# Gathers of 127 and 125 rows, and PSUM operands for VectorE, in a two-layer graph kernel

## The reference

```
# layer 0
m     = relu(x[src] + edge_attr)                       # 400000 x 32
neigh = segment_sum(m, dst, num_segments=12500)
x     = layernorm(x + (1 + eps) * x + neigh)
# layer 1
x_s   = x * rsqrt(clip(out_degree, 1))[:, None]
agg   = segment_sum(x_s[src], dst, num_segments=12500)
x     = layernorm(x + agg * rsqrt(clip(in_degree, 1))[:, None])
```

## Time and profile before

| | |
|---|---|
| time, median of 2 runs | 6580.52 us (6580.47 to 6580.58) |
| the profiled execution | 6585.29 us, span 6583.5 us |
| first layer, to the end of its sums | 0 to 4763 us |
| norm between the layers | 4763 to 4820 us |
| second layer's sums | 4820 to 6540 us |
| final norm and output | 6540 to 6584 us |
| GpSimd (POOL) busy | 5088.2 us, 77% |
| VectorE (DVE) busy | 2819.4 us, 43% |
| TensorE (PE) busy | 2745.2 us, 42% |
| ScalarE (ACT) busy | 1588.2 us, 24% |
| mean granted TensorE clock | 0.684 |

### The profile page before, as it was taken

One profiled execution on the slowest core, in us unless ns is written; L12 is line 12 of the kernel. 1 busy time (PEld: TensorE's weight loads), 2 busy tenths in 40 slices (PEclk: granted clock), 3 DMA queues, 4 the chain that ended last, 5 costly groups with the idle time before them and its releaser, 6 DMA issues. The chain is left out here.

```text
span 6583.5 us, 68332 instructions
## 1 busy us (share of the span) xinstructions
PE 2745.2 (42%) x22843; PEld 2292.8 (35%) x22843; DVE 2819.4 (43%) x4668; ACT 1588.2 (24%) x2158; POOL 5088.2 (77%) x4335
## 2 busy tenths in 40 slices
PE   2222222222222222222222222222358888888887
PEld 2222222222222222222222222222347676666665
DVE  5233232232232232332232332332367777777776
ACT  0000000000000000000000000000068888888885
POOL 7787787787787787787787787787767777777773
PEclk7555555555555555655555655655679999999998
DMA  2111111111111111111111111111111111111111
GB/s 45 24 21 22 24 21 21 24 21 21 24 21 22 24 21 22 24 21 22 24 21 22 24 21 22 24 21 22 18 38 19 19 19 18 19 18 19 18 19 28
DMA packets 246365, 147.86 MB, mean 22 GB/s; under 512 B 159963, under 2 KB 229164, under 8 KB 245804
## 3 DMA queue, kind: packets, MB, share of 16 engines
q0 software_dynamic: 138400, 80.97, 9.0%
q1 hardware_dynamic: 107940, 66.58, 4.1%
HBM read 141.61 MB, written 5.61 MB: 22 GB/s over the span
## 5 line engine op out<-in xcount | busy, mean ns | idle before, releaser
L133 POOL DMA_INDIRECT rows<-in_x,src_t x3125 | 3796.8, 1215 | 957.6 <-issue 952.0
L380 PE MATMUL agg<-dst_hot,msg 128*33 128x128 f32 x6250 | 943.4, 326 | 2487.5 <-ACT msg L364 2487.5
L380 PEld LDWEIGHTS agg<-dst_hot,msg 128*33 128x33 f32 x6250 | 831.2, 136 | 2593.4 <-ACT msg L364 2514.5
L133 POOL DMA_INDIRECT rows<-table,src x1200 | 1279.1, 1066 | 387.2 <-issue 377.5
L578 ACT ACTIVATE counts<-built 128x686 bf16<-128x686 f32 x1925 | 1452.8, 984 | 261.8 <-PE built L603 252.0
L364 ACT ACTIVATE msg<-edge_t 128x800 f32<-128x800 f32 (+1 forms) x126 | 108.9, 864 | 4602.8 <-DVE edge_t L297 4602.8
L297 DVE TENSOR_TENSOR edge_t<-edge_t,rows 128x800 f32<-128x800 f32 (+1 forms) x126 | 125.5, 996 | 2109.0 <-DMA rows<-in_x,src_t 2109.0
L603 PE MATMUL built<-key_hot,hi_hot 128*128 128x343 bf16 x3850 | 930.5, 325 | 103.5 <-ACT counts L578 56.7
L622 PE MATMUL applied<-counts,x_parts 128*96 128x175 bf16 x7546 | 913.7, 246 | 0.9 <-ACT prod L583 0.9
L622 PEld LDWEIGHTS applied<-counts,x_parts 128*96 128x96 bf16 x7546 | 786.3, 128 | 152.9 <-ACT counts L578 1.0
L376 PE MATMUL hist<-lo_hot,hi_hot 128*128 128x98 bf16 x3125 | 277.8, 283 | 1003.5 <-DVE lo_hot L288 1003.5
(11 more groups left out here) (109 smaller groups left out, 702.6 us busy)
## 6 DMA issues: line engine op xcount, KB each, us to landing
edge_t<-in_edge_attr SPq DMA_DIRECT2D x125, 400.0 KB
rows<-in_x,src_t POOLq DMA_INDIRECT x3125, 2.4
rows<-table,src POOLq DMA_INDIRECT x1200
src_t<-in_src SPq DMA_DIRECT2D x125, 12.5 KB
dst_t<-in_dst SPq DMA_DIRECT2D x125, 12.5 KB
base_t<-in_dst SPq DMA_DIRECT2D x125, 0.5 KB
x<-x SPq DMA_DIRECT2D x1, 1568.0 KB
x<-in_x SPq DMA_DIRECT2D x1, 1372.0 KB
```

The costliest lines, as they stand in the source:

```text
L133: gp.indirect_dma_start(rows_d[:, j, :], None, nodes, bass.IndirectOffsetOnAxis(ap=src_d[:, j:j + 1].bitcast(U32), axis=0),).then_inc(s, 16)
L380: last = te.matmul(agg[:, :], msg[:, j, :], dst_hot[:, j, :], start=(j == 0), stop=(j == J - 1))
```

## The change

**First layer.** Groups 0 to 124 take M0 = 127 partitions (3175 edges), one last group, the 126th, takes M1 = 125 (3125 edges); every gather, comparison, addition and product of a group is on that many partitions. VectorE's comparisons read their integer row from PSUM (`iota_ps`, a copy made once) and not from SBUF. A ScalarE copy puts the group's edge rows into PSUM (`edge_ps`, signalled by `s_edge`), and the edge addition reads them there; it still writes into `edge_t`. The edge rows are loaded by two DMAs (partitions 0 to 111 and the rest), so `s_in` counts to 80 a group.

**Second layer.** NG = 80 groups of 16 gathers of 125 rows (160000 edges), and NC = 75 counted groups (240000 edges). `LAST` becomes 80. Since gathers now outlast the counted groups, waits for `l_moved` go by the helper `moves`. The comparisons there keep both operands in SBUF.

```diff
-    NG = 3 * J
-    NC = G - NG * JG // J
-    CE0 = NG * JG * P
+    M0, M1 = P - 1, P - 3
+    G0 = E // (M0 * J)
+    GE0, LAST0 = M0 * J, E - G0 * M0 * J
+    NG = 80
+    CE0 = NG * JG * M1
+    NC = (E - CE0) // GE
...
-            sp.dma_start(edge_d.rearrange("p j d -> p (j d)"),
-                         edge[bass.ds(e0, GE), :].rearrange("(p j) d -> p (j d)", p=P)).then_inc(s, 16)
+            for p0, p1 in bands:
+                sp.dma_start(edge_d[p0:p1, :, :].rearrange("p j d -> p (j d)"),
+                             edge[bass.ds(e0 + p0 * J, (p1 - p0) * J), :].rearrange("(p j) d -> p (j d)", p=p1 - p0)).then_inc(s, 16)
...
                 gp.indirect_dma_start(
-                    rows_d[:, j, :], None, nodes,
-                    bass.IndirectOffsetOnAxis(ap=src_d[:, j:j + 1].bitcast(U32), axis=0),
+                    rows_d[0:m, j, :], None, nodes,
+                    bass.IndirectOffsetOnAxis(ap=src_d[0:m, j:j + 1].bitcast(U32), axis=0),
...
+                iota_ps = pb("iota_ps")[:, 0:P]
+                edge_ps = own.enter_context(nc.psum_tensor("edge_ps", [P, 1024], F32))[:, 0:J * D].rearrange("p (j d) -> p j d", d=D)
+                s_edge = sem("s_edge")
...
+                    V(ve.tensor_copy(iota_ps, iota[:, :]))
...
+                            row = iota_ps[0:m, :].unsqueeze(1).to_broadcast([m, J, P])
...
-                            ve.tensor_tensor(hi_hot[:, :, :], tiles_of(iota[:, :], J), last_dim(s_hi[:, :], P), ALU.is_equal).then_inc(s_v, 1)
+                            ve.tensor_tensor(hi_hot[0:m, :, :], row, last_dim(s_hi[0:m, :], P), ALU.is_equal).then_inc(s_v, 1)
...
-                            ve.tensor_tensor(lo_hot[:, :, :], tiles_of(iota[:, :], J)[:, :, 0:C], last_dim(s_lo[:, :], C), ALU.is_equal).then_inc(s_v, 1)
-                            ve.tensor_tensor(dst_hot[:, :, :], tiles_of(iota[:, :], J), last_dim(rel[:, :], W), ALU.is_equal).then_inc(s_v, 1)
+                            ve.tensor_tensor(lo_hot[0:m, :, :], row[:, :, 0:C], last_dim(s_lo[0:m, :], C), ALU.is_equal).then_inc(s_v, 1)
+                            ve.tensor_tensor(dst_hot[0:m, :, :], row, last_dim(rel[0:m, :], W), ALU.is_equal).then_inc(s_v, 1)
...
+                                    ve.wait_ge(s_edge, g + 1)
...
-                                piece = edge_t[:, slot, j0:j1, :]
-                                ve.tensor_tensor(piece, piece, rows[:, slot, j0:j1, :], ALU.add).then_inc(s_v, 1)
+                                ve.tensor_tensor(edge_t[0:m, slot, j0:j1, :], edge_ps[0:m, j0:j1, :], rows[0:m, slot, j0:j1, :], ALU.add).then_inc(s_v, 1)
...
+                            sc.wait_ge(s_in[slot], (i + 1) * 80)
+                            sc.activation(edge_ps[0:m, :, :], edge_t[0:m, slot, :, :], ACT.Copy).then_inc(s_edge, 1)
...
-                            gathers(gp, 0, JG, table[:, :], rows[:, slot, :, :], src_t[:, slot, :], l_rows[slot])
+                            gathers(gp, M1, 0, JG, table[:, :], rows[:, slot, :, :], src_t[:, slot, :], l_rows[slot])
...
+            def moves(k):
+
+                return min(k - 1, NC + 1) if isinstance(k, int) else k - 1
```

More of the change, by code:

```diff
@@ L38, in build @@
     HS = [n * SPAN for n in HT]
-    assert G * GE == E and G % 2 == 1 and NC <= P and C % 2 == 0 and CE0 + NC * GE == E and CE0 % GE == 0
+    assert LAST0 == M1 * J and G0 % 2 == 1 and NC <= P and C % 2 == 0 and CE0 + NC * GE == E and CE0 % GE == 0
     assert 0 < TAIL <= C and HK <= 512 and max(HS) <= P and J % CH == 0 and J - 1 <= C and KEYS <= J * NC
@@ L180, in both @@
                     for slot in range(2):
-                        step(i, slot, i * 2 + slot)
-                step(turns, 0, G - 1)
+                        step(i, slot, i * 2 + slot, M0)
+                step(turns, 0, G0 - 1, M0)
+                step(turns, 1, G0, M1)
             with ExitStack() as own:
@@ L343, in _, with step @@
                             gp.iota(pick_i[:, h, :], [[1, max(HT)], [0, SPAN]], base=h * HT[0], channel_multiplier=0).then_inc(s_const, 1)
-                        def step(i, slot, g):
-                            gp.wait_ge(s_in[slot], (i + 1) * 64)
+                        def step(i, slot, g, m):
+                            gp.wait_ge(s_in[slot], (i + 1) * 80)
                             gp.sem_inc(s_mark, 1)
-                            n = PIECES[0][1] if isinstance(g, int) else J
-                            gathers(gp, 0, n, x[:, :], rows[:, slot, :, :], src_t[:, slot, :], s_rows[slot])
+                            n = PIECES[0][1] if m == M1 else J
+                            gathers(gp, m, 0, n, x[:, :], rows[:, slot, :, :], src_t[:, slot, :], s_rows[slot])
                             if n < J:
-                                gathers(gp, n, J, x[:, :], rows[:, slot, :, :], src_t[:, slot, :], s_late)
+                                gathers(gp, m, n, J, x[:, :], rows[:, slot, :, :], src_t[:, slot, :], s_late)
                         both(gp, step)
@@ L371, in _, with step @@
                         prepare_pe(te)
-                        def step(i, slot, g):
+                        def step(i, slot, g, m):
                             te.wait_ge(s_v, g * VG + (v0 + 6))
                             for j in range(J):
-                                te.matmul(hist[:, :], hi_hot[:, j, :], lo_hot[:, j, :], start=False, stop=False)
-                            for n, (j0, j1) in enumerate(PIECES if isinstance(g, int) else [(0, J)]):
+                                te.matmul(hist[:, :], hi_hot[0:m, j, :], lo_hot[0:m, j, :], start=False, stop=False)
+                            for n, (j0, j1) in enumerate(PIECES if m == M1 else [(0, J)]):
                                 te.wait_ge(s_a, g + (len(ROUNDS) + 1 + n))
                                 for j in range(j0, j1):
-                                    last = te.matmul(agg[:, :], msg[:, j, :], dst_hot[:, j, :], start=(j == 0), stop=(j == J - 1))
+                                    last = te.matmul(agg[:, :], msg[0:m, j, :], dst_hot[0:m, j, :], start=(j == 0), stop=(j == J - 1))
                             last.then_inc(s_agg, 1)
@@ L477, in step @@
                                 sp.wait_ge(l_hot, g - 1)
[L478 removed]
+                            load_indices(sp, g * (JG * M1), M1, JG, src_t[:, slot, :], dst_t[:, slot, :], base_t[:, slot, :], l_in[slot])
                         each(sp, step, NG - 1)
@@ L503, in dst_hots @@
                             def dst_hots(j0, j1):
-                                return ve.tensor_tensor(dst_hot[:, j0:j1, :], tiles_of(iota_b[:, :], j1 - j0),
-                                                        last_dim(rel[:, j0:j1], W), ALU.is_equal)
+                                return ve.tensor_tensor(dst_hot[0:M1, j0:j1, :], tiles_of(iota_b[:, :], j1 - j0)[0:M1, :, :],
+                                                        last_dim(rel[0:M1, j0:j1], W), ALU.is_equal)
                             def chunk(q):
@@ L611, in step @@
                                         te.wait_ge(l_added, k - 1)
-                                        te.wait_ge(l_moved, k - 1)
+                                        te.wait_ge(l_moved, moves(k))
                                     for j in range(JG):
-                                        last = te.matmul(agg[:, :], rows[:, other, j, :], dst_hot[:, j, :], start=(j == 0), stop=(j == JG - 1))
+                                        last = te.matmul(agg[:, :], rows[0:M1, other, j, :], dst_hot[0:M1, j, :], start=(j == 0), stop=(j == JG - 1))
                                     last.then_inc(l_sum, 1)
@@ L639, in _ @@
                         te.wait_ge(s_v, V.n - 1)
-                        PE(te.matmul(small[0:1, 0:1], outside[:, :], ones[:, :], start=True, stop=True))
+                        PE(te.matmul(small[0:1, 0:1], outside[0:M1, :], ones[0:M1, :], start=True, stop=True))
                 general_sums(1, table[:, :], CH, D3, (src_t, dst_t, rows, rel, dst_hot, agg), None, None)
@@ L680, in _ @@
                             gp.sem_inc(s_mark, 1)
-                            gathers(gp, 0, n, nodes, rows[:, 0, :, :], src_t[:, 0, :], g_rows)
+                            gathers(gp, P, 0, n, nodes, rows[:, 0, :, :], src_t[:, 0, :], g_rows)
                 @block.vector
```

83 lines of the change are left out of this document (41 added, 42 removed).

## The result

The changed kernel takes 12365.65 us (median of 2 runs, 12364.58 to 12366.72) against 6580.52 (6580.47 to 6580.58): 1.879 times the time before, 95% interval 1.871 to 1.887. It is slower, far outside the forecast of 5785 us and its range.

A forecast was written before the change was run, and what follows sets the result against it. GpSimd's gathers were taken to bound both layers, many held by VectorE. The terms -806 - 23 + 58 - 28 = -799 us led from 6580.5 to 5785 us, 12% faster; range 5120 to 5880, the forecast's own 5740 to 5860.

The forecast's parts named there:

- What bounds the kernel: Both layers: GpSimd's gathers set the pace; 847 us of the first layer is gathers held by VectorE.
- Part 1: First layer: one PSUM operand in comparisons and edge addition ends the hold on gathers, -806 us.
- Part 2: Gathers of 127 and 125 rows, priced by rows: -23 us in the first layer, -28 in the second.
- Part 3: Second layer's split: five more gather groups cost +105 us, a shorter end gives -47, together +58.
- A: Rival: gathers of 127 or 125 rows are much cheaper than of 128, giving 4900 to 5400 us; chance 0.32.
- B: Rival: one DMA engine, always the same, takes all rows of a gather; about 8760 us; chance 0.05.
- C: Rival: gathers stay held although an operand is in PSUM; 6625 us, no change; chance 0.07.
- the points that would show the prediction wrong: Gathers beside hi_hot still over 2 us, or, second, a gather's own price over 1.11 us.

The follow-up runs named there:

- e1: Kernel before with only the comparisons' integer row and the edges in PSUM, all gathers 128 rows: 5748.02 us against 6585.56, ratio 0.8722.
- e10: Same kernel as e1, run again on another chip: 5746.34 us, 0.8723 of the kernel before.
- e11: Kernel before with only the comparisons' integer row in PSUM, edges added in SBUF, on the chip of e10: 5833.64 us, 0.8848 of the kernel before.
- e3: Kernel of 128 rows with PSUM operands, plus an unused probe gather of one of 25 row counts after each first-layer gather in full groups: 10464.84 us.
- e12: The changed kernel's second layer behind the first layer of e10: 6133.45 us, 0.9302 of the kernel before.
- e8: Same kernel as e11, on another chip: 8218.67 us against 7540.20 for the kernel before there, ratio 1.091.
- e5: The kernel of e3 with all 25 probe gathers of 113 rows: 15632.94 us.
- e9: Changed kernel with a group's gathers posting to two semaphores in turn, five and five: 11167.70 us.
- e6: Changed kernel with an already met wait and a semaphore increment before every fifth gather as well: 12369.11 us.

## Why the prediction was wrong

**What bounds the kernel: right.** GpSimd's gathers set the pace before and after, and their whole growth is the growth of the time.

**Part 1: right.** It said 806 us for 126 groups; by the same working 125 groups have 3125 x 1.250 + 10 = 3916 against 4754, 838 us, and e1 and e10 gave 838 and 845. The hold went with one operand in PSUM, the comparisons kept their 3.5 us, and the ScalarE copy was hidden, as argued. The edge addition's share of the gain is 87 us (e11). The Trainium skill's inference in "SBUF — State Buffer", "Who interferes with whom", that tensor_tensor does not stall the generation of DMA descriptors, does not carry over to these gathers: e10 got 838 us back. What the prediction took from the same section of the Trainium skill, that two SBUF inputs contend with a GpSimd instruction that reads SBUF, agrees. Whether a held gather waits to read its row numbers or to write its descriptors, no run tells.

**Part 2: the step that failed.** "No row shows a gather of another count. ... From above: nothing saved, 0.944. By rows: 127/128 gives 0.937 and 125/128 gives 0.922. ... I take the price by rows, nearest to the only count seen". Measured are 2.548 and 1.207 (e3 alone: 2.548 and 1.198). Three errors lie in it. First, the price does not go by a gather's rows but by those of its fullest engine, m/k: 127 where 128 had 8 (e3). Second, the unknown price was bounded from above by 0.944, with one sentence that a loss was not excluded. Nothing in the trace bounded it: 32 packets a gather, two an engine, were in the earlier trace rows, and the prediction itself drew from them that an odd count may be laid out over fewer engines. It then read that as a saving. The same fact says that 8 rows in 16 equal shares cannot be had with 127. Third, the pauses: 1205 us, in no row of before, where a group's stretch had 25 x 9 = 225 entries.

By terms: the first layer's gathers were predicted at 3150 x (0.937 + 0.306) + 10 = 3925 us and took 3150 x (2.540 + 0.306) + 1205 = 10170, 6245 over. The second layer was predicted 30 us longer and is 365 longer. Together 6580 of the 6581 us by which the forecast was off.

**Part 3: right, as far as the runs tell.** Five more groups and a shorter end were +58 at the old price per gather, with 47 us back at the end; e12 has 47 back. Of e12's 394 us, 1280 x (1.330 - 1.058) = 348 are the price of a gather, which leaves 46 for the split, 12 less than predicted; no run changes the split alone. The remark that the second layer's mean stays some 0.12 over its median holds too (1.315 to 1.207); that its bf16 comparisons, with both inputs in SBUF, are the reason was not tested.

**Rivals.** A: the layout over fewer engines is real, its sign is wrong. B had the right direction and the right first fact, one engine takes all the rows; its price and condition are wrong. It wanted a DMA engine as the bound, with fewer than two in turn, and gave 8760; in fact the engines idle between gathers, and GpSimd pays. The reason for dismissing it fails too: that the transfers go to engines in turn, which that section of the Trainium skill states, hides the engines' time and not GpSimd's. C falls by e1. Of the points that would show the prediction wrong, the second was met, a gather of over 1.11 us: (7999.6 + 1683.4)/4430 = 2.19. That a rise of 0.17 us in a price never seen loses everything was written down there, and should have been a rival with a chance of its own.

## What to carry to other kernels

Take indirect gathers from GpSimd with a row count that is 9 or fewer for each of 14 to 16 engines: 128, 126, 120 and 112 cost 0.93 to 0.99 us here, 127 costs 2.55; where a count doesn't divide, filling it up with repeated rows should do it, which no run here tried. To speed up GpSimd's gathers beside VectorE, give VectorE's long two-input instructions one operand in PSUM: 838 us here, without touching the rows, as long as no other engine then sets the pace (e8). And where a change alters the shape of the one instruction that bounds the kernel, its price is the open question, so bound it from above by what each engine's share would be in the worst layout, not by the old price.

## What the runs showed of the hardware

- A gather on GpSimd costs 0.837 + 0.0134 us for each row on the fullest of its DMA engines (e3, 25 counts). Engines without rows get as many 4-byte transfers: 25 MB of them in the changed kernel.
- When gathers in a row that post to one semaphore add up to about 1000 entries an engine (between 993 and 1024, counting one for the completion), GpSimd pauses, 3.5 us behind gathers of 127 rows and 2.5 behind 128 and 113 in turn (e5). It goes on 0.93 us (e5: 1.04) after the last packet issued so far has ended. A change of the semaphore prevents it (e9), an already met wait does not (e6).
- A gather that starts in a VectorE comparison or addition with two SBUF inputs is held (3.62 us beside hi_hot in the earlier trace rows, 1.69 in e11); with one operand in PSUM it takes 0.94 or 0.95 us (e10, e11).
- A VectorE comparison of 127 or 128 x 3200 elements takes 3.48 to 3.49 us whether its broadcast operand is in SBUF or PSUM.
